# The diagonal block of a tile read by GpSimd and ScalarE, and two chunks folded in one VectorE operation

## The reference

```python
h = jnp.maximum(_layernorm(x, axis=-1), 0.0)          # x: 8192 x 512
mask = incidence_m > 0                                # incidence_m = adj: 8192 x 8192
head = mask / jnp.maximum(jnp.sqrt(jnp.sum(mask * mask, axis=-1, keepdims=True)), EPS)
inc = incidence_m + head
edge_fea = inc @ h
edge_degree = jnp.sum(inc, axis=-1, keepdims=True)
x = x + edge_fea / edge_degree
```

## Time and profile before

| | us |
|---|---|
| median of 3 runs (1267.59 to 1268.84) | 1268.14 |
| the profiled execution's own time | 1278.49 |
| its span | 1276.7 |
| VectorE busy in the span | 1189.2 (93%) |
| ScalarE busy | 975.5 (76%) |
| TensorE busy | 959.0 (75%) |
| GpSimd busy | 791.1 (62%) |
| bytes moved by DMA | 471.00 MB, mean 369 GB/s |

### The profile page before, as it was taken

How to read it: one execution, slowest core, us unless ns; L and a number is a source line. 1 busy time by engine, 2 the same in 40 slices (tenths; PEclk the granted TensorE clock), 3 DMA queues, 4 the chain that set the end, 5 groups by cost and what they waited for, 6 DMA issues and landing times.

```text
span 1276.7 us, 14660 instructions
## 1 busy us (share of the span) xinstructions
PE 959.0 (75%) x2680; PEld 478.1 (37%) x2682; DVE 1189.2 (93%) x2868; ACT 975.5 (76%) x1902; POOL 791.1 (62%) x748
## 2 busy tenths in 40 slices
PE   0003878888888878787988887978878888977677
PEld 0001434444444444443434443434444434433343
DVE  6679999998999999998999999999999999999961
ACT  6657787887887988786888877888877888884731
POOL 1003667676666777776766767777776776765562
PEclk9999899898988989899898989999989988987888
DMA  9999999999999999999999999999999999997532
GB/s 356 427 422 406 396 394 388 369 387 369 379 378 382 401 373 401 395 401 394 402 400 401 392 374 384 399 400 395 402 396 402 402 397 373 401 390 275 175 106 74
DMA packets 148207, 471.00 MB, mean 369 GB/s; under 512 B 24826, under 2 KB 24826, under 8 KB 143965
## 3 DMA queue, kind: packets, MB, share of 16 engines
q1 hardware_dynamic: 90368, 331.38, 66.3%
q0 software_dynamic: 57744, 138.64, 29.7%
HBM read 490.47 MB, written 33.82 MB: 411 GB/s over the span
## 4 chain that ended last, share of the span: by engine, by line
DVE 55%; issue 17%; DMA 11%; ACT 6%; PE 6%; another core or an unknown queue 2%; SPq 1%; POOL 0%; DVEq 0%; ACTq 0%; POOLq 0%
DVE cand_word L794 17%; DVE folded L772 16%; DMA adj_tile<-in_adj_dram 8%; DVE cand_index L798 6%; DMA gathered_rows<-in_x_dram 3%; PE acc L1326 3%; DVE cand_index L817 2%; DVE cand_word L812 2%; ACT junk L573 2%; ACT adj_tile L560 2%; ACT diag L636 1%; PE acc L1337 1%; DVE diagonal_alone L779 1%; DVE entry L961 1%
## 5 line engine op out<-in xcount | busy, mean ns | idle before, releaser
L494 POOL DMA_INDIRECT gathered_rows<-h_scratch,slot_column x520 | 559.9, 1077 | 263.1 <-issue 158.0
L573 ACT ACTIVATE junk<-adj_tile,zero_unit 128x2048 bf16<-128x2048 f32 x256 | 510.0, 1998 | 48.3 <-issue 27.5
L1326 PE MATMUL acc<-gathered_rows,diag 128*128 128x512 f32 x1040 | 489.6, 622 | 21.4 <-DMA gathered_rows<-h_scratch,slot_column 18.2
L494 POOL DMA_INDIRECT gathered_rows<-h_scratch,spill_column x198 | 223.1, 1127 | 195.0 <-ACT spill_column L619 135.2
L794 DVE MAX8 cand_word<-folded 128x8 f32<-128x1024 f32 x244 | 298.2, 1222 | 5.9 <-remote 1.3
L772 DVE SCALAR_TENSOR_TENSOR folded<-adj_tile 128x1024 f32<-128x1024 f32 x244 | 296.1, 1214 | 7.7 <-DMA adj_tile<-in_adj_dram 5.6
L1326 PEld LDWEIGHTS acc<-gathered_rows,diag 128*128 128x128 f32 x1040 | 203.8, 204 | 263.4 <-issue 262.6
L798 DVE FIND_INDEX8 cand_index<-cand_word,folded 128x8 uint32<-128x1024 f32 x244 | 297.3, 1219 | 0.0
L1337 PE MATMUL acc<-gathered_rows,spill_matrix 128*128 128x512 f32 x396 | 186.8, 609 | 46.0 <-DMA gathered_rows<-h_scratch,spill_column 42.4
L636 ACT ACTIVATE diag<-ident,weights_and_payload 128x128 f32<-128x128 f32 x581 | 176.2, 388 | 16.0 <-issue 6.5
L1337 PEld LDWEIGHTS acc<-gathered_rows,spill_matrix 128*128 128x128 f32 x396 | 72.8, 192 | 154.8 <-issue 154.6
(11 more groups left out here) (151 smaller groups left out, 880.1 us busy)
## 6 DMA issues: line engine op xcount, KB each, us to landing
adj_tile<-in_adj_dram SPq DMA_DIRECT2D x256, 1024.0 KB
h_scratch<-adj_tile SPq DMA_DIRECT2D x16, 1024.0 KB, 10.6
out_dram<-out_tile SPq DMA_DIRECT2D x64, 256.0 KB
gathered_rows<-in_x_dram SPq DMA_DIRECT2D x12, 1024.0 KB, 12.6
x_residual<-in_x_dram SPq DMA_DIRECT2D x48, 256.0 KB
gathered_rows<-h_scratch,slot_column POOLq DMA_INDIRECT x520
x_held<-in_x_dram SPq DMA_DIRECT2D x4, 1024.0 KB, 7.9
gathered_rows<-h_scratch,spill_column POOLq DMA_INDIRECT x198, 3.5
```

The lines of the kernel that those rows point to most:

```text
L494: nc.gpsimd.indirect_dma_start(out=into, out_offset=None, in_=h[:, :], in_offset=bass.IndirectOffsetOnAxis(ap=column, axis=0), bounds_chec ...
L573: nc.scalar.activation(junk[:, n % 2].rearrange("p (j c) -> p j c", j=2), both[:, :, half], ACT.Relu, bias=zero_unit[:], scale=-UP, accum_ ...
L1326: last = nc.tensor.matmul(acc[t % 3][:], diag[:, t % 2, 1 + s], slot(t % 2, s), start=False, stop=False)
```

## The change

GpSimd multiplies the diagonal block by the identity (`read_diagonal`, now a `tensor_tensor` into `picked`, between `gather_spill(t-2)` and `gather_own(t)`, for tile t+1). ScalarE sums it at the head of its next period (`sum_diagonal`). VectorE's `keep_diagonal` waits for that sum (`diag_summed`) and stands behind the first `find_places`, just ahead of `counts`. SyncE's wait `diag_read` is now for GpSimd's operation. `fold` takes two chunks in one operation of 2048 elements and writes both halves of F, so it waits for both chunks and for the last search of F ahead of it. The folds that stood between `take_entry` and `columns_any`, and between `heads` and `incs`, are gone.

```diff
--- before.py
+++ after.py
@@ -385,7 +386,7 @@
-                        sp.wait_ge(folded, CHUNKS * (t - 2) + j + 1)
+                        sp.wait_ge(folded, 2 * (t - 2) + j // 2 + 1)
                         if j == diag_chunk(t - 2):
                             sp.wait_ge(diag_read, t - 1)
@@ -513,9 +514,19 @@
+            def read_diagonal(t):
+                pool.wait_ge(adj_loaded[t % 2][diag_chunk(t)], 16 * turn(t))
+                if t >= 1:
+                    pool.wait_ge(diag_summed, t)
+                nc.gpsimd.tensor_tensor(picked[:], diagonal(chunk(t % 2, diag_chunk(t))[:, diag_half(t)], t), ident[:],
+                                        ALU.mult).then_inc(diag_read, 1)
+
+            read_diagonal(0)
             for b in range(4):
                 pool.wait_ge(h_stored[b], 16 * (LN // 4))
+            read_diagonal(1)
             gather_own(0)
+            read_diagonal(2)
             gather_own(1)
             for t in range(2, BATCH + 1):
...
                 gather_spill(t - 2)
+                if t + 1 < FOLDED:
+                    read_diagonal(t + 1)
                 gather_own(t)
@@ -670,6 +683,11 @@
+            def sum_diagonal(t):
+                act.wait_ge(diag_read, t + 1)
+                nc.scalar.activation(picked[:], picked[:], ACT.Copy,
+                                     accum_out=on_diag[:, t:t + 1]).then_inc(diag_summed, 1)
...
                 small, pay, pick, end = p >= 0, q >= 0, r >= 0, f >= 0
+                if 0 <= p < FOLDED:
+                    sum_diagonal(p)
                 check_any(t, 0)
@@ -764,31 +784,27 @@
-            def fold(t, j):
-                dve.wait_ge(adj_loaded[t % 2][j], 16 * turn(t))
-                if CHUNKS * t + j >= 2:
-                    dve.wait_ge(idx_found, CHUNKS * t + j - 1)
-                a = chunk(t % 2, j)
-                nc.vector.scalar_tensor_tensor(out=F[:, j % 2], in0=a[:, 1], scalar=UP, in1=a[:, 0],
+            def fold(t, k):
+
+                for j in (2 * k, 2 * k + 1):
+                    dve.wait_ge(adj_loaded[t % 2][j], 16 * turn(t))
+                if 2 * t + k >= 1:
+                    dve.wait_ge(idx_found, CHUNKS * t + 2 * k)
+                a = A[:, t % 2, 4 * CW * k:4 * CW * (k + 1)].rearrange("p (j h c) -> p j h c", j=2, h=2)
+                nc.vector.scalar_tensor_tensor(out=F[:], in0=a[:, :, 1], scalar=UP, in1=a[:, :, 0],
                                                op0=ALU.mult, op1=ALU.add).then_inc(folded, 1)
-                if j == diag_chunk(t):
-                    read_diagonal(t)
+                if k == diag_chunk(t) // 2:
                     cut_diagonal(t)
 
-            def read_diagonal(t):
-                nc.vector.scalar_tensor_tensor(out=picked[:], in0=diagonal(chunk(t % 2, diag_chunk(t))[:, diag_half(t)], t),
-                                               scalar=1.0, in1=ident[:], op0=ALU.mult, op1=ALU.mult,
-                                               accum_out=on_diag[:, t:t + 1]).then_inc(diag_read, 1)
...
             def keep_diagonal(t):
-                dve.wait_ge(diag_read, min(t, FOLDED - 1) + 1)
+                dve.wait_ge(diag_summed, min(t, FOLDED - 1) + 1)
@@ -974,15 +990,14 @@
                 if small:
                     values(p)
-                    keep_diagonal(p)
                 if pick:
                     find_entry(r)
                 find_places(t, 0)
                 if small:
+                    keep_diagonal(p)
                     counts(p)
                 if pick:
                     take_entry(r)
-                fold(t, 1)
                 if small:
                     columns_any(p)
                     ranks(p)
@@ -995,12 +1010,11 @@
-                fold(t, 2)
+                fold(t, 1)
                 find_values(t, 2)
                 find_places(t, 2)
                 if small:
                     heads(p)
-                fold(t, 3)
                 if small:
                     incs(p)
                 find_values(t, 3)
```

5 lines of the change are left out of this document (3 added, 2 removed).

## The result

The changed kernel took 1276.89 us (median of four runs, 1275.23 to 1278.24), the kernel before 1267.87 us on the same chip: a ratio of 1.0062, 95% interval 1.0047 to 1.0077. It is slower by 0.6%, some 8 us. The forecast was 1269.6 and no change. The result is 0.9 us above the range's upper end of 1276, and at it (1276.0) if the ratio is put on the 1268.14 that the forecast started from. All profiles of the changed kernel here are of an execution of 1275.23 us, span 1273.5.

What follows compares the result with a forecast made beforehand. VectorE and the DMA engines were taken to be full at once. VectorE's -2.6, the start's +2.3 and the late two-chunk wait's +1.8 sum to +1.5 us on 1268.14: 1269.6 us, no change, range 1261 to 1276.

Steps and rivals of the forecast that it cites:

- The VectorE sum: VectorE over 61 tiles: removed read, merged folds and new dependences come to -2.6 us, between +4.7 and -17.
- `read_diagonal` away: VectorE: the removed diagonal read saves 0.31 us a tile, -18.9 us over 61 tiles.
- Merge: VectorE's folds: one instruction less a pair saves 0.06 us, -7.3 us over 122 pairs, engine's rate an element unchanged.
- Cut next to the fold: VectorE: the cut right behind its fold costs +0.13 us in 48 tiles, +6.2 us.
- Reciprocal next to its reader: VectorE: heads directly ahead of incs costs 0.19 us against 0.06, +7.8 us over 60 tiles.
- Copy next to the counts: VectorE: keep_diagonal directly ahead of counts, 0.25 us against 0.06, +11.4; middle with the heads-incs case's +7.8 taken: +9.6 us.
- The start: Tile 1 on VectorE must wait for its second chunk: between 0 and 4.6 us, +2.3 taken.
- the race: Loads run ahead of VectorE, their lead melts and is used up by about 980 us, capping VectorE's gain.
- The wait for two chunks, late: Late folds on VectorE: the third fold waits for chunk 3 too, once, between 0 and +4.5 us, +1.8 taken.
- loads decide, slower: Rival, chance 0.26: plain runs used up the loads' lead, VectorE's saving is worth nothing: 1273 us, to 1276.
- Hidden on GpSimd: GpSimd's multiply, 0.5 us taken (0.3 to 1.3), fits in its 2.75 us wait: cost 0.
- The release of the diagonal's chunk: Loads of chunks 0 and 1 wait some 3.6 us later in 32 tiles; cost 0, up to +3.

Runs made afterwards that it cites:

- offload_only: The kernel before with GpSimd and ScalarE reading the diagonal as in the change, four single folds, copy at its old place: 1269.04 us, ratio 1.0005.
- merged_respaced: The change with other work put between VectorE's operations and what they wait for, copy back behind values: 1307.44 us, ratio 1.0306 to the kernel before.
- offload_respaced: The kernel before with the diagonal on GpSimd and ScalarE, four single folds, one small operation between each fold and its reader: 1268.76 us, ratio 1.0.
- offload_respaced_2: The same kernel as offload_respaced, run again: 1268.96 us, ratio 1.0 to the kernel before.
- before_again: The kernel before, unedited, run and profiled a second time: 1267.79 us, ratio 0.9996.
- after_copy_back: The change with the copy of the diagonal value moved back ahead of find_entry: 1273.23 us, ratio 1.0042 to the kernel before.
- merge_only: The kernel before with two merged folds a tile, VectorE still reading the diagonal, copy at its old place: 1272.47 us, ratio 1.0028.
- after_split: The change with each fold of 2048 elements made as two operations of 1024, on the second chip: 1289.83 us, ratio 1.0056 to the kernel before.
- offload_respaced_light: Diagonal on GpSimd and ScalarE, single folds, one operation between fold and reader, without the 48 x loads, second chip: 1250.79 us, 0.9747 to the kernel before.

## Why the prediction was off

The time came out at the upper end of the range, 0.9 us above it as measured and at 1276.0 by the ratio; the direction (no change) was not met.

**The VectorE sum, -2.6 us, is the step that failed.** By its terms, over 61 tiles:
- `read_diagonal` away: -18.9, as forecast (offload_only, 0.31 less 0.13 a tile, 0.19 measured).
- Merge: 0.04 a pair where 0.06 was taken, -4.9 for -7.3. The reasoning (a little fixed cost saved, same rate an element) held.
- Cut next to the fold: 2.33 - 2.20 = 0.13, +6.2, as forecast.
- Reciprocal next to its reader: 0.18 - 0.06 = 0.12, +7.3 for +7.8.
- Copy next to the counts: 0.25 - 0.06 = 0.19, +11.6 for +9.6. The row of the same adjacency, 1226.51 to 1226.76, had the right number; the prediction took a middle with a milder case.
- **Not in the sum: the merged fold's wait for the search just ahead of it**, 0.14 a tile, +8.5. The prediction looked for new dependences on results that an operation reads, and not for the one on the buffer that it writes, although the change's text says that the fold waits for the last search of F.

With it the sum is -18.9 - 4.9 + 6.2 + 7.3 + 11.6 + 8.5 = +9.8, where the periods give +9.7. The test of it is merged_respaced, which begins at 16.65 us with the cut, the reciprocal, the copy and the first fold's wait taken apart, and whose second fold keeps its wait. That the time still came out near the range is luck: the sum was wrong by 12.4 us, and about half of it was paid out of waits that the prediction had not counted on.

**The start**: +2.3 forecast, +2.7 measured. Right.

**Loads.** The prediction saw the race and that a gain would be capped, and it was: offload_only, offload_respaced and offload_respaced_2 arrive at 1.000 with a VectorE up to 25 us faster. What it left open, whether plain runs also have those waits, decides the size: before_again has 8.9 us of them. So of the changed kernel's +9.8 and +2.7, 12.5 us, 8.9 - 2.3 = 6.6 replace waits, and 5.9 remain; tile 60 came 1116.3 - 1111.1 = 5.2 us later. The profiled spans differ by 5.0, the medians by 9.0, and the ratio stands for 7.8. The 4 us between come from which executions were profiled: before_again's is the slowest of its 11 (1270.22, median 1267.79), the changed kernel's the fastest of its four (1275.23, median 1276.89). What is different in the others no trace shows.

**The wait for two chunks, late**: +1.8 forecast. after_copy_back gives about +3 at the limit of the loads. In the changed kernel little of it can be seen, as VectorE had fallen behind the loads (2.3 us of waits). So the rival "loads decide, slower" has the right size by accident: its mechanism would have given about 1272, what after_copy_back shows, and the rest is VectorE's own slowing.

**GpSimd and ScalarE.** The multiply took 0.53 us (0.5 taken; the bounds were 0.3 and 1.3) and was hidden. The Trainium skill, "GPSIMD Engine Reference", section 3.1, would have it near an estimated 0.28 us beside the dispatch; the trace has 525 ns as the mean of 61. The groups by line, of the changed kernel:

```profile
L495 POOL DMA_INDIRECT gathered_rows<-h_scratch,spill_column x198 | 264.5, 1336 | 95.3 <-issue 67.2 <-ACT spill_column L632 27.5 <-DVE slot_column L897 0.3
L521 POOL TENSOR_TENSOR diagonal_alone<-adj_tile,ident 128x128 f32<-128x128 f32 x61 | 32.1, 525 | 91.9 <-DMA adj_tile<-in_adj_dram 90.6
```

The spill gathers are 1336 ns in the mean where they were 1127 before. GpSimd's timeline shows why, and that no wait is left in this turn of the changed kernel (it had 2.75 us):

```profile
599.41 2.19 POOL L495 DMA_INDIRECT gathered_rows<-h_scratch,slot_column  x1 [0.30 <-issue]
...
608.46 2.05 POOL L495 DMA_INDIRECT gathered_rows<-h_scratch,spill_column  x1 [0.30 <-issue]
610.52 0.53 POOL L521 TENSOR_TENSOR diagonal_alone<-adj_tile,ident 128x128 f32<-128x128 f32 x1
611.21 1.04 POOL L495 DMA_INDIRECT gathered_rows<-h_scratch,slot_column  x1 [0.16 <-issue]
```

Both long gathers began inside one of the two folds shown above, and end 0.87 and 0.88 us after it (598.44 + 2.29 = 600.73 to 601.60; 609.63 to 610.51). Unheld, GpSimd's turn is eleven gathers at 1.3 us and 0.69 us of the multiply up to the next one, 15.0 us; the held time fills the other 2.2. In tiles 16 to 31 and 48 to 60 that is all; in the others up to 0.7 us a tile of idle time is left. "Hidden on GpSimd" held for the change as it is: no wait on VectorE is put down to GpSimd or to ScalarE, and after_copy_back, with as much time held (136 us), has a period 0.2 us shorter. But the cover is nearly used up, and with VectorE's order of merged_respaced it is gone, at +3%. The prediction took an indirect DMA for 1.0 us; the trace that it read already had 108 longer ones, held for 65 us in all, and it didn't ask what a longer fold does to them.

**The release of the diagonal's chunk** came later, as forecast: SyncE's row is

```profile
SPq L391 <- POOL diagonal_alone L521: 221.4, 30, 15.7
```

30 waits, the longest 15.7 us, for GpSimd. offload_only has the same late release (30 waits, the longest 14.0 us) and reaches tile 60 at 1109.9, before_again at 1111.1: cost 0, as taken.

## What to carry to other kernels

When two operations on two half buffers become one on the whole buffer, look for what it now waits for on both sides, the readers of what it overwrites included, and price every pair that becomes adjacent by a row where the same pair already stands adjacent. Before summing an engine's gain, find out whether it waits for loads in more than one execution: at such a limit neither a gain nor a loss of the engine passes through in full (25 us faster gave 0 here, 12.5 us slower gave 5 to 9). And an engine "with 20% idle" may have no slack in its turn (GpSimd is busy 160 of 200 us in the changed kernel): sum its turn, with what other engines add to it, before giving it work.

## What the runs showed of the hardware

**Indirect DMAs wait for VectorE's running fold.** In all of before, the changed kernel, merge_only, merged_respaced, offload_respaced and after_split, each of the indirect DMAs over 1.15 us (108, 119, 119, 115, 132 and 49 of 721) began while a fold with two SBUF inputs was running, and ended 0.87 us after that fold (at most 1.07); one that began ahead of a fold wasn't lengthened. No fold was lengthened in the runs where GpSimd had gathers alone. The time above 1.0 us each comes to 65 us in the first profile of before (44 in before_again), 136 in the changed kernel, 158 in merge_only, 176 in merged_respaced, 87 in offload_respaced and 40 in after_split. The longer the fold, the larger the part of a period in which a gather can be caught and the longer it is held.

**GpSimd's multiply and VectorE's operations with two SBUF inputs hold each other.** Of the 61 multiplies of offload_only, 24 began inside a fold; they took up to 1.56 us where the others take 0.53, and ended 0.37 us after the fold. VectorE paid as well: 32 of its operations that overlapped a multiply were lengthened, by 7.3 us in all, in offload_respaced_light 37, by 8.1 us, in after_split 29 cuts, by 0.2 us each. All were operations with two SBUF inputs (folds, cuts, `incs` and their like). MAX8 and FIND_INDEX8, with one such input, overlapped multiplies 47 and 26 times in offload_only and were never lengthened by more than 0.06 us. In the changed kernel no multiply met a fold or a cut, and each took 0.51 to 0.54 us; one other operation of VectorE was lengthened, by 0.3 us.

The Trainium skill, "SBUF — State Buffer", section "Who interferes with whom", has a VectorE instruction with two SBUF inputs contend with a GpSimd instruction that reads SBUF. The multiplies agree with it. The same section infers, from a `tensor_tensor`, that the making of descriptors isn't stopped by such an operation; here the gathers were held by folds with two SBUF inputs, and only that side waited: the measurement decides.

**A short operation costs more when the next one reads its result**, by start to start: 0.06 against 0.18 us for a reciprocal of 128x1, 0.06 against 0.25 for a copy of 128x1, 1.12 against 1.25 and 2.20 against 2.33 for the folds; and 0.06 to 0.08 more when what follows waits for a search that ended one or two short operations before. For the small operations the extra is as large as what they cost otherwise, or larger, and the four kinds that this change adds made 33.6 us over the 61 tiles (6.2 + 7.3 + 11.6 + 8.5).
